# Reciprocal roots on GpSimd, and the causal mask in VectorE's minimum: a fused retention, attention and expert layer

## The reference, cut to what matters

```
x = x + Attn1(layernorm(x))      # 16 heads of 8: rotary, causal with decay, no softmax, per-head norm
x = x + Attn2MoE(layernorm(x))

# in Attn2MoE:
h = rms(x) ; q = rms(heads(wq)) ; k = rms(heads(wk)) ; v = heads(wv)      # 16 heads of 8
scores = q k^T / sqrt(8);  scores = where(causal, scores, -inf);  attn = softmax(scores)
x = x + (attn v) wo^T            # first 32 channels of the addend set to 0
moe = 4 experts of rms(x), weighted by the two largest gate values
```

## Time and profile before

| | us |
|---|---|
| median of 3 runs (1178.98 to 1180.13) | 1179.03 |
| the profiled execution | 1180.29 |
| its span in the trace | 1178.1 |
| PE busy with matmuls | 945.5 (80%), 6192 instructions |
| DVE busy | 602.3 (51%), 1483 instructions |
| ACT busy | 499.6 (42%) |
| POOL busy | 314.5 (27%) |
| maxima reductions on DVE (L852), 256 | 211.2 |
| mask matmuls on PE (L359), 512 | 85.2 |

### The profile page before, as it was taken

How to read it: one execution, slowest core, us unless ns; L and a number is a source line. 1 busy time by engine, 2 the same in 40 slices (tenths; PEclk the granted TensorE clock), 3 DMA queues, 4 the chain that set the end, 5 groups by cost and what they waited for, 6 DMA issues and landing times.

```text
span 1178.1 us, 16413 instructions
## 1 busy us (share of the span) xinstructions
PE 945.5 (80%) x6192; PEld 570.6 (48%) x6192; DVE 602.3 (51%) x1483; ACT 499.6 (42%) x1008; POOL 314.5 (27%) x538
## 2 busy tenths in 40 slices
PE   2845768878798888988799888988888888988857
PEld 1625535534545455554556455554555453544434
DVE  2544565565753566465663566455653574245021
ACT  1314215245445444444445445454445343524524
POOL 4203104213412232133412232133412220311311
PEclk9576657676789776986788776986789767857959
DMA  4000000000000000000000000000000000000000
GB/s 138 1 9 1 1 9 2 1 1 10 1 1 1 19 1 1 2 10 10 1 1 2 19 1 1 1 11 1 1 1 2 10 1 0 11 1 1 10 1 10
DMA packets 13726, 9.05 MB, mean 8 GB/s; under 512 B 2128, under 2 KB 13136, under 8 KB 13648
## 3 DMA queue, kind: packets, MB, share of 16 engines
q1 hardware_dynamic: 13648, 8.00, 2.3%
HBM read 5.64 MB, written 2.10 MB: 7 GB/s over the span
## 4 chain that ended last, share of the span: by engine, by line
PE 64%; DVE 25%; ACT 5%; issue 4%; POOL 1%; DMA 0%; SPq 0%; POOLq 0%; ACTq 0%; DVEq 0%
PE side L456 13%; PE side L343 9%; PE outs L394 7%; DVE mneg L852 7%; PE side L444 6%; PE scores L374 6%; PE maxima L356 5%; PE side L492 4%; PE side L414 4%; PE maxima L359 4%; PE outs L432 3%; PE side L439 3%; ACT p L637 2%; DVE hB L993 2%; DVE p L862 2%
## 5 line engine op out<-in xcount | busy, mean ns | idle before, releaser
L852 DVE TENSOR_REDUCE mneg<-maxima 128x2 f32<-128x256 f32 (+3 forms) x256 | 211.2, 825 | 321.3 <-PE maxima L359 319.6
L637 ACT ACTIVATE p<-scores 128x1024 f32<-128x1024 f32 (+3 forms) x256 | 180.1, 704 | 188.7 <-PE scores L374 187.5
L1079 POOL TENSOR_SCALAR_AFFINE_SELECT p<-p 128x256 f32<-128x256 f32 x256 | 106.9, 417 | 526.9 <-ACT p L637 526.8
L356 PE MATMUL maxima<-ks,qs 24*128 24x384 f32 (+3 forms) x512 | 110.8, 429 | 102.0 <-DVE mneg L852 101.7
L374 PE MATMUL scores<-qs,ks 25*128 25x256 f32 (+3 forms) x512 | 129.0, 501 | 20.5 <-ACT p L637 18.2
L356 PEld LDWEIGHTS maxima<-ks,qs 24*128 24x128 f32 x512 | 61.5, 237 | 131.5 <-DVE mneg L852 128.5
L394 PE MATMUL outs<-p,v2x 128*32 128x512 f32 (+3 forms) x1024 | 115.2, 587 | 1.0 <-POOL p L1079 1.0
L374 PEld LDWEIGHTS scores<-qs,ks 25*128 25x128 f32 x512 | 57.1, 219 | 100.0 <-issue 60.6
L359 PE MATMUL maxima<-negb,idb 128*128 128x128 bf16 x512 | 85.2, 258 | 0.0
L1087 POOL TENSOR_SCALAR_AFFINE_SELECT p<-p 128x512 f32<-128x512 f32 x64 | 41.0, 641 | 165.3 <-ACT p L646 165.3
L414 PE MATMUL side<-qs,ks 24*128 24x128 f32 x512 | 58.9, 334 | 23.7 <-DVE p L862 20.6
(11 more groups left out here) (169 smaller groups left out, 1528.0 us busy)
## 6 DMA issues: line engine op xcount, KB each, us to landing
x_in<-x_dram SPq DMA_DIRECT2D x8, 256.0 KB, 2.9
qs<-mT SPq DMA_DIRECT2D x128, 2.0 KB
out_dram<-yout SPq DMA_DIRECT2D x8, 256.0 KB, 2.3
sb_t_cos<-t_cos_dram SPq DMA_DIRECT2D x1, 512.0 KB, 4.8
sb_t_sin<-t_sin_dram SPq DMA_DIRECT2D x1, 512.0 KB, 5.0
sb_w_l<-w_l_dram SPq DMA_DIRECT2D x2, 256.0 KB
sb_w_qkv<-w_qkv_dram SPq DMA_DIRECT2D x2, 192.0 KB, 3.6
sb_w_u<-w_u_dram SPq DMA_DIRECT2D x3, 128.0 KB
```

The source lines that it names most:

```text
L356: nc.tensor.matmul(mb[:, i, 0:n + 128], qs[rows, b % 2, g, n:n + 128], ks[rows, b % 2, g, 0:n + 128], start=True, stop=False, skip_group_c ...
L637: A_(p2[kt][:, 2 * hp:2 * hp + 2, :], eb[:, :, 0:n], ACT.Exp, scale=float(D) ** -0.5).then_inc(exp_done, 1)
L852: V.tensor_reduce(mneg[:, g, 2 * hp:2 * hp + 2, qt], mb[:, :, 0:128 * (qt + 1)], AX.X, ALU.max, negate=True)\
L1079: Q.affine_select(out=diag, in_=diag, compare_op=ALU.is_ge, fill=0.0, base=0, pattern=[[0, 2], [1, 128]], channel_multiplier=-1).then_inc( ...
```

## The change

Three things are changed.

1. The roots move. VectorE only computes the variance plus epsilon and raises `var_ready`; GpSimd raises it to the power -0.5 in one instruction (`root`) and raises `root_ready`; VectorE waits for that before it uses the result. To leave room for this the steps of many pieces are moved later: the use of `norm1` from step 4 to 5, of `pre` from 9 to 11 and 12, of `norm2` from 16 to 19, of `tail` from 25 to 27, and the transposes and projections behind them by one to three steps.
2. The mask moves. TensorE no longer adds it. VectorE takes each head by an instruction of its own that reads the head's scores in PSUM and a tile `negx` in SBUF (zeros, and in the last 128 columns the mask), writes `-(score + mask)` back to PSUM and accumulates its minimum into `mneg`. `m_filled` now counts heads, so that the first head can be taken while the second is in the array.
3. The masked scores of the first layer are issued in pairs of positions j, alternating between two PSUM banks and two groups of array rows.

```diff
-    NF + 5: [(1, "ON")],
+    NF + 7: [(1, "ON")],
+    NF + 8: [(1, "WO1")],
-    NF + 10: [(1, "H")],
+    NF + 13: [(1, "H")],
...
-        idb = sb("idb", [128, 128], bf16)
-        negb = sb("negb", [128, 128], bf16)
+        negx = sb("negx", [128, T])
...
-            scratch[name] = (sb("rv_" + name, [128, n]), sb("ri_" + name, [128, n], i32), sb("ry_" + name, [128, n]),
-                             sb("rt_" + name, [128, n]))
+            scratch[name] = (sb("rv_" + name, [128, n]), sb("ry_" + name, [128, n]))
+        mhalf = sb("mhalf", [128, 1])
...
-        m_filled = counted("m_filled", G * GK)
+        m_filled = counted("m_filled", 2 * G * GK)
...
+        var_ready = {name: counted("var_ready_" + name) for name in scratch}
+        root_ready = {name: counted("root_ready_" + name) for name in scratch}
...
                     nc.tensor.matmul(mb[:, i, 0:n + 128], qs[rows, b % 2, g, n:n + 128], ks[rows, b % 2, g, 0:n + 128],
-                                     start=True, stop=False, skip_group_check=True)
-                for i in range(2):
-                    last = nc.tensor.matmul(mb[:, i, n:n + 128], idb[:], negb[:], start=False, stop=True, skip_group_check=True)
-                last.then_inc(m_filled, 1)
+                                     start=True, stop=True).then_inc(m_filled, 1)
...
-                for j in range(J):
-                    dst = side(f"SC{t}{j}", b)
-                    rows = slice(SW * j, SW * j + SHIFT)
+                for pair in ((0, 1), (2, 3)):
+                    dst = [side(f"SC{t}{j}", b) for j in pair]
                     for g in range(G):
-                        last = nc.tensor.matmul(dst[:, 128 * g:128 * g + 128], ks1[rows, g, at], qs1[rows, g, at],
-                                                start=True, stop=True)
-                    last.then_inc(side_filled, 1)
+                        for j in pair:
+                            rows = slice(SW * j, SW * j + SHIFT)
+                            last = nc.tensor.matmul(dst[j % 2][:, 128 * g:128 * g + 128], ks1[rows, g, at], qs1[rows, g, at],
+                                                    start=True, stop=True)
+                            if g == G - 1:
+                                last.then_inc(side_filled, 1)
...
-            def rsqrt(name):
-
-                v, i, y, t = (a[:] for a in scratch[name])
-                step(V.tensor_scalar(i, v.bitcast(i32), 1, None, ALU.logical_shift_right))
-                step(V.tensor_scalar(y.bitcast(i32), i, -1, RSQRT_SEED, ALU.mult, ALU.add))
-                for _ in range(3):
-                    step(V.tensor_tensor(t, y, y, ALU.mult))
-                    step(V.scalar_tensor_tensor(t, t, -0.5, v, ALU.mult, ALU.mult))
-                    step(V.scalar_tensor_tensor(y, t, 1.5, y, ALU.add, ALU.mult))
...
-                dve.wait_ge(m_filled, count(m_filled, b, k + 1))
                 if k % GK == 0 and b:
                     dve.wait_ge(mT_ready, count(mT_ready, b - 1, g + 1))
-                V.tensor_reduce(mneg[:, g, 2 * hp:2 * hp + 2, qt], mb[:, :, 0:128 * (qt + 1)], AX.X, ALU.max, negate=True)\
-                    .then_inc(max_read, 1)
+                n = 128 * (qt + 1)
+                for i in range(2):
+                    dve.wait_ge(m_filled, count(m_filled, b, 2 * k + i + 1))
+                    at = V.tensor_tensor_reduce(out=mb[:, i, 0:n], in0=mb[:, i, 0:n], in1=negx[:, T - n:T], scale=-1.0, scalar=FMAX,
+                                                op0=ALU.add, op1=ALU.min, accum_out=mneg[:, g, 2 * hp + i, qt:qt + 1])
+                at.then_inc(max_read, 1)
 
             def masked(b, t, j):
...
-                rv, _, ry, _ = scratch["norm1"]
-                if s == 2:
+                rv, ry = scratch["norm1"]
+                if s == 3:
                     dve.wait_ge(o1_squared, count(o1_squared, b, 1))
                     step(V.tensor_reduce(red[:], hB[:, 0, :].rearrange("p (h d) -> p h d", d=D), AX.X, ALU.add))
-                    step(V.tensor_scalar(rv[:], red[:], 1.0 / D, EPS_LN, ALU.mult, ALU.add))
-                if s == 3:
-                    rsqrt("norm1")
-                if s == 4:
+                    V.tensor_scalar(rv[:], red[:], 1.0 / D, EPS_LN, ALU.mult, ALU.add).then_inc(var_ready["norm1"], 1)
+                if s == 5:
+                    dve.wait_ge(root_ready["norm1"], count(root_ready["norm1"], b, 1))
                     V.tensor_tensor(nat[:].rearrange("p t (h d) -> p (t h) d", d=D), o1[:].rearrange("p t (h d) -> p (t h) d", d=D),
                                     bc(ry[:], D), ALU.mult).then_inc(nat_ready, 1)
-                if s == 7:
...
                     step(i)
-                    step(V.tensor_scalar(rv[:], red2[:], 1.0 / D, EPS_RMS, ALU.mult, ALU.add))
-                if s == 15:
-                    rsqrt("norm2")
-                if s == 16:
+                    V.tensor_scalar(rv[:], red2[:], 1.0 / D, EPS_RMS, ALU.mult, ALU.add).then_inc(var_ready["norm2"], 1)
+                if s == 19:
+                    dve.wait_ge(root_ready["norm2"], count(root_ready["norm2"], b, 1))
                     for n in (1, 0):
...
+            def root(b, name):
+
+                rv, ry = scratch[name]
+                pool.wait_ge(var_ready[name], count(var_ready[name], b, 1))
+                Q.tensor_tensor(ry[:], rv[:], mhalf[:].broadcast_to([128, rv.shape[1]]), ALU.pow).then_inc(root_ready[name], 1)
+
             def before(b, s):
-                if s in (12, 13):
-                    m = s - 12
+                if s == 3:
+                    root(b, "norm1")
+                if s == 10:
+                    root(b, "pre")
...
-            sp.dma_start(p[:, 0:128], A["t_neg"]).then_inc(masks_loaded, 16)
+            sp.dma_start(negx[:, T - 128:T], A["t_neg"]).then_inc(masks_loaded, 16)
```

More of the change, by code:

```diff
@@ L47 @@
     NF + 1: [(1, "N1"), (-1, "MT3")],
[L48 to L51 removed]
+    NF + 2: [(-2, "DN1")],
+    NF + 4: [(2, "XN"), (-2, "DN2")],
+    NF + 6: [(-2, "DN3")],
+    NF + 7: [(1, "ON")],
+    NF + 8: [(1, "WO1")],
     NF + 9: [(0, "MT0")],
[L53 to L55 removed]
+    NF + 13: [(1, "H")],
+    NF + 14: [(1, "Q20"), (1, "Q21")],
+    NF + 15: [(1, "Q22"), (1, "Q23")],
     NF + 17: [(0, "MT1")],
[L57 to L62, removed]
[L63 to L66 removed]
+    NF + 20: [(-1, "N20"), (-1, "N21"), (2, "Q10"), (2, "Q11")],
+    NF + 21: [(2, "Q12"), (2, "Q13")],
+    NF + 22: [(1, f"S21{g}") for g in range(G)] + [(-1, "AO")],
+    NF + 23: [(1, f"S20{g}") for g in range(G)],
+    NF + 24: [(-1, "WO2")],
+    NF + 25: [(0, "MT2")],
+    NF + 26: [(2, "QT")],
+    NF + 27: [(2, "ST")],
+    NF + 28: [(2, f"S10{g}") for g in range(G)],
+    NF + 29: [(-1, "XF")],
+    NF + 30: [(2, f"S11{g}") for g in range(G)] + [(-1, "GATE")],
 }
@@ L789, in _ @@
                 for place in range(NF):
+                    if place == 0 and on(it - 2):
+                        tail(it - 2, G * GK)
                     if place in (0, 3, 5) and on(it + 1):
@@ L807, in _ @@
                         maxima_transposed(it + MT_AT[s][0], MT_AT[s][1])
+                    if s in (28, 30) and on(it + 2):
+                        lead(it + 2, s)
                     if on(it - 1):
                         tail(it - 1, s)
-                    if on(it + 2):
+                    if s not in (28, 30) and on(it + 2):
                         lead(it + 2, s)
@@ L928, in before @@
                     moments(x1[:, b % 3], 1)
-                rv, _, ry, _ = scratch["pre"]
-                if s == 8:
+                rv, ry = scratch["pre"]
+                if s == 10:
                     step(V.tensor_scalar(rv[:, 0:NT], mv[:, 1, :, 1], EPS_LN, None, ALU.add))
-                    step(V.scalar_tensor_tensor(rv[:, NT:2 * NT], rv[:, 0:NT], EPS_RMS, mv[:, 1, :, 1], ALU.mult, ALU.add))
-                    rsqrt("pre")
-                if s == 9:
+                    V.scalar_tensor_tensor(rv[:, NT:2 * NT], rv[:, 0:NT], EPS_RMS, mv[:, 1, :, 1], ALU.mult, ALU.add)\
+                        .then_inc(var_ready["pre"], 1)
+                if s == 11:
+                    dve.wait_ge(root_ready["pre"], count(root_ready["pre"], b, 1))
                     for t in range(NT):
@@ L944, in before @@
                     i.then_inc(z_ready, 1)
-                rv, _, ry, _ = scratch["norm2"]
-                if s == 14:
+                rv, ry = scratch["norm2"]
+                if s == 17:
                     for m in range(2):
@@ L979, in lead @@
                 if s == 4 - NF:
-                    step(V.tensor_scalar(rv[:], mv[:, 0, :, 1], EPS_LN, None, ALU.add))
-                    rsqrt("lead")
+                    V.tensor_scalar(rv[:], mv[:, 0, :, 1], EPS_LN, None, ALU.add).then_inc(var_ready["lead"], 1)
                 if s == 6 - NF:
+                    dve.wait_ge(root_ready["lead"], count(root_ready["lead"], b, 1))
                     for t in range(NT):
@@ L1023, in tail @@
```

(19 more changed lines are left out.)

131 lines of the change are left out of this document (71 added, 60 removed).

## The result

The changed kernel takes 1315.03 us (1314.66 to 1317.09, 4 runs) against 1179.58 us (1178.98 to 1181.97, 4 runs) before: 1.115 times, interval 1.113 to 1.117. It is 135 us slower; forecast were 1105 us and a range of 1050 to 1185.

What follows compares the result with a forecast made beforehand. TensorE was taken as the bound, with some 18 us per pass standing still. Masks -39, roots -34, pipeline ends -6, fused minimum +9 and pairs -5 made -75 us against 1180.29: 1105 us; eight-of-ten range 1050 to 1185.

Steps and rivals of the forecast that it cites:

- moved steps: Pieces moved to later steps: a longer path only at the pipeline's filling and emptying, inside the 6 us for these ends.
- I take the tenfold price: it is hidden, for all five: Roots on GpSimd: a power at ten times a product's rate per element, 2.9 us for `norm2`, hidden; bounds 0.5 and 27 us.
- The power on GpSimd is dear: Rival: VectorE stands at `root_ready`, TensorE behind its maxima; at 100 times a product's price 1265 us and more; chance 0.12.
- The room: Time for `norm2` on GpSimd before its use: two steps of maxima at 3.3 us each, so 6.6 us.
- The mask products: Mask pairs leave TensorE: 0.22 us in each of 178 steps, 39 us gained; ends 20 and 70 us.
- The clock falls: Rival: without the mask products' full-array work TensorE's granted clock goes from 0.78 to 0.70 in a pass, 1175 us; chance 0.11.
- The fused minimum: VectorE's minimum for two heads: 1.15 us, 0.33 us more a step; 9 us lost, ends 25 gained and 140 lost.
- The roots' departure: 440 small instructions leave VectorE: TensorE's stalls behind them go, 34 us gained; ends 10 and 101.7 us.
- The pairs: First layer's masked scores in pairs of banks: 0.15 us for each of 32 blocks, 5 us gained; ends 10 lost, 25 gained.
- The collision of the sine products: Sine products on VectorE against the cosine product on GpSimd, 3.07 us for two products: stays, both again in the same steps.
- the signs named ahead: Profile after: power 0.3 to 3 us, unwaited; maxima wait near 70 us; pair 1.15 us; VectorE near 579 us; clock 0.74 to 0.80.

Runs made afterwards that it cites:

- mask_only: The kernel before with only the mask moved to VectorE's fused minimum; old roots, steps and order of masked scores: 1191.5 us, 1.009 times.
- all_back: The changed kernel with all five roots on VectorE and the masked scores in the old order: 1155.4 us, 0.978 times.
- prod_oldpairs: root_as_product with the masked scores in the old order; reciprocal roots left out: 1063.1 us, 0.899 times.
- root_as_product: The changed kernel with GpSimd's power replaced by a product with 0.0001, so the reciprocal roots are left out: 1087.9 us, 0.921 times.
- roots_only: The changed kernel with the mask back on TensorE and the masked scores in the old order; roots on GpSimd and moved steps stay: 1337.4 us, 1.132 times.
- prod_pemask: prod_oldpairs with the mask back on TensorE and VectorE's single reduction; reciprocal roots left out: 1070.7 us, 0.906 times.
- norms_back: The changed kernel with norm1 and norm2 by eleven steps on VectorE, three small powers on GpSimd, masked scores in the old order: 1142.7 us, 0.967 times.
- norms_back_pemask: norms_back with the mask back on TensorE and the single reduction: 1148.2 us, 0.970 times.
- half_norm2: The changed kernel, masked scores in the old order, with half of norm2's power replaced by a product with 0.0001: 1214.0 us, 1.027 times.
- pairs_only: The kernel before with only the first layer's masked scores issued in pairs: 1199.7 us, 1.015 times.
- norms_two: norms_back with two Newton steps instead of three for norm1 and norm2: 1129.6 us, 0.956 times.
- act_norms: The changed kernel, masked scores in the old order, norm1 and norm2 on ScalarE as exp(-0.5 ln v), small roots on GpSimd: 1090.2 us, 0.922 times.

## Why the prediction was wrong, point by point

The runs make a ledger from before to after. Each line is the difference of two medians:

| part | forecast, us | measured, us | from |
|---|---|---|---|
| mask off TensorE, fused minimum | -39 + 9 = -30 | +10 | before, mask_only |
| moved steps | in the ends | -36 | mask_only, all_back |
| roots off VectorE, GpSimd's part at a product's price | -34 - 6 = -40 | -92 | all_back, prod_oldpairs |
| pairs in the masked scores | -5 | +25 | prod_oldpairs, root_as_product |
| the power's duration | 0 (hidden) | +227 | root_as_product, after |
| sum | -75 | +134 | |

The ledger is one way through the edits, and its lines are not prices that hold beside any neighbour. By them roots_only would take 1181 - 36 - 92 + 227 = 1280 us; it took 1337. The move of the mask lost 10 us in mask_only and gained 8 between prod_pemask and prod_oldpairs, 5 or nothing beside large roots on VectorE, and some 41 to 47 by estimate beside the power. One reason can be seen in the traces. The passes in the middle take few lengths, whatever TensorE's busy time: 119.5 us in root_as_product, 126.3 in all_back, norms_back and norms_back_pemask, 133.1 in the kernel before, mask_only and half_norm2, 146.8 in the changed kernel and 153.6 in roots_only, each 6.8 us or twice that from the next; in prod_oldpairs, prod_pemask, pairs_only, norms_two and act_norms they vary. An edit that stays within one length shows at the ends alone. What sets these lengths no run shows.

- **The step that failed** is "I take the tenfold price: it is hidden, for all five". The price was 20.7 us for `norm2`, not 2.9: the power per element is 77 times a product. It lay inside the bounds (0.5 to 27 us), beside the rival "The power on GpSimd is dear", whose mechanism came true: VectorE stands at the semaphore and TensorE behind it, at `norm2` for L1020 and not for the maxima. Between ends 50 times apart I had chosen by nearness to a product, though nothing in the trace computed a power; the rival's chance of 0.12 was too low. The Trainium skill ("GPSIMD Engine Reference", section "4.1 Engine selection") puts products of two inputs on GpSimd at about half of VectorE's speed. For products the trace before agrees, 1.27 us against 0.68 us for 512 elements (L1153, L958); it gives no price of a power.
- **The room** was wrong as well: 6.6 us by the mean step of a pass, 2.0 us in the trace, since the two steps there hold short reductions that VectorE had ready. Both errors go one way. With the measured price and my room, 1105 + 8 x (20.7 - 6.6) + 8 x (10.5 - 6.6) = 1249; with the room of 2.0 us for both, 1105 + 8 x 18.7 + 8 x 8.5 = 1323, close to 1315.
- **The mask products** (-39): too large, and with the wrong sign in the kernel before. The 0.22 us for each step were real as starts in the timeline. In the middle passes of mask_only waits took them back, at an unchanged clock of 0.79; over the whole run its mean clock was lower, 0.743 against 0.764, and with cheap roots 0.793 against 0.816. The rival "The clock falls" had that direction right for these two pairs. It does not hold for all: beside the power the kernel without mask products has the higher clock (0.729 against 0.720). How much of the 22 us is clock alone no run separates.
- **The fused minimum**: a pair takes 1.00 us, not 1.15, against 0.825 for the one reduction. The overlap that I had named for the lower end is there, though not whole. VectorE's busy time fits: 602.3 - 106 + 256 x (1.00 - 0.825) = 541, measured 543.9; I had 579. The Trainium skill's rule ("VectorE: DVE Perf Modes", section "Two Vector instructions with no wait between them") did count rightly: four instructions stand in the trace. At my fixed part for each it was 0.47 us longer; the trace shows 0.18, since the reads lie beside streaming.
- **The roots' departure** was worth more than forecast, 92 us and not 40, near the upper end that I had named (101.7). The stall of 2.35 us behind `norm2` was only the part in one row; with the chains gone, the waits of TensorE's maxima for VectorE fall from 101.7 to 40.3 us in root_as_product.
- **The pairs** (-5): wrong sign. I had seen that the first bank would be complete later, and took the loads beside each other to outweigh it. What I left out is that the second pair waits for two banks before its first product.
- **The collision of the sine products** was to stay: it did not, and the moved steps, which I had counted only at the ends, are worth 36 us.
- Of the signs named ahead: the power at 0.3 to 3 us, no wait for it and the pair at 1.15 us failed; the clock in a pass (0.77) stood between 0.74 and 0.80. The wait for maxima, 83.8 us in 39 instances, says little, since the stall shows mainly behind other instructions of VectorE (L1020, L961).

The sum without the power would have been fair by luck: 1087.9 measured against 1105, out of terms that missed by 30 to 52 us in both directions.

## What to carry to other kernels

Before an operation moves to another engine, have one row of that very operation on that engine, at its size; a relative in the same instruction form can be 77 times cheaper. When something is to be hidden, count the microseconds between its start and its consumer's arrival in the timeline at that place, not in mean steps. And work that leaves the bounding engine pays only where nothing else becomes due there: here 81 to 86 us of TensorE's products brought anything from a loss of 10 us to a gain of 8, and by estimate over 40 beside a long stall. So test an edit beside the neighbours that it will have: differences of runs do not simply add up.

## What the runs showed of the hardware

- A power on GpSimd: 1.02, 1.64, 10.5 and 20.7 us for 4, 8, 64 and 128 elements on 128 partitions, some 160 ns each. The product of 128 takes 0.40 us.
- The fused add-and-minimum on VectorE: heads of 512 columns follow each other in 0.61 to 0.65 us; the read of the accumulator (0.14 us) costs nothing where another head follows.
- ScalarE: 1.283 us for the load of the logarithm's table and as much for the way back, 0.31 us for each activation of 128 elements. A reciprocal root as exp(-0.5 ln v) takes 3.2 us in all.
- TensorE's mean granted clock was lower without mask products in three pairs of kernels (0.793 and 0.816; 0.743 and 0.764; 0.755 and 0.773) and higher in the changed kernel than in roots_only, which has them (0.729 and 0.720; the order of the masked scores differs too).
